# An attention and mixture-of-experts layer: each head's scores in a row group of 32 partitions, the first batch projected straight into it, shift rows in half batches

## The reference

```
x: (8, 256, 128)      16 heads of 8, 8 experts, 2 of them per token
Q, K, V = x @ Wq + bq, x @ Wk + bk, x @ Wv + bv        per batch, 16 heads
attn = softmax(Q K^T / sqrt(8))                        per head, 256 x 256
x = layernorm(x + (attn V) @ Wo + bo)
shared = (silu(x @ sw1) * (x @ sw3)) @ sw2             width 256
gates = the two largest of sigmoid(x @ router_w.T) + bias, normalised
routed = sum over e of gates[e] * gelu(x @ ew1[e]) @ ew2[e]   8 experts, width 128
out = layernorm(x + shared + routed)
```

## Time and profile before

| | |
|---|---|
| median of three runs | 265.02 us (263.12 to 265.13) |
| profiled execution, its span | 261.9 us |
| between its span and the median | 3.1 us |
| PE, PEld busy | 225.9, 158.7 us |
| DVE, ACT, POOL busy | 186.1, 152.3, 119.1 us |
| chain that ended last | PE 59%, DMA 13%, DVE 11%, POOL 6% |

### The profile page before, as it was taken

One profiled execution on the slowest core, in us unless ns is written; L12 is line 12 of the kernel. 1 busy time (PEld: TensorE's weight loads), 2 busy tenths in 40 slices (PEclk: granted clock), 3 DMA queues, 4 the chain that ended last, 5 costly groups with the idle time before them and its releaser, 6 DMA issues.

```text
span 261.9 us, 4502 instructions
## 1 busy us (share of the span) xinstructions
PE 225.9 (86%) x1546; PEld 158.7 (61%) x1546; DVE 186.1 (71%) x370; ACT 152.3 (58%) x292; POOL 119.1 (45%) x186
## 2 busy tenths in 40 slices
PE   1766984999999999994999999997999899999850
PEld 1434854667677677772676766655767576767520
DVE  8953893777969879794269762348567796976953
ACT  1440722576666667663356678866696468665620
POOL 8677381000100007130448988435319977273511
PEclk9995885899999999999589999999979999999995
DMA  7277864405528082476000000069980495792111
GB/s 191 53 92 91 86 69 98 40 11 86 45 53 77 23 85 30 78 53 228 3 0 5 3 5 5 4 108 140 226 143 28 94 147 84 129 161 74 40 40 40
DMA packets 16198, 19.43 MB, mean 74 GB/s; under 512 B 1280, under 2 KB 11712, under 8 KB 16032
## 3 DMA queue, kind: packets, MB, share of 16 engines
q1 hardware_dynamic: 15744, 18.49, 43.4%
q0 software_dynamic: 144, 0.39, 1.0%
q10 hardware_dynamic: 288, 0.27, 0.6%
HBM read 11.22 MB, written 1.11 MB: 47 GB/s over the span
## 4 chain that ended last, share of the span: by engine, by line
PE 59%; DMA 13%; DVE 11%; POOL 6%; issue 5%; ACT 3%; SPq 1%; POOLq 0%; DVEq 0%; ACTq 0%
PE ring L818 17%; PE pv_bank L832 14%; PE max_bank L804 12%; DMA kstack<-gate_scratch 6%; DMA qstack<-top_rows 4%; POOL qstack L522 3%; DVE kstack L629 3%; DVE probs_mem L737 2%; DMA kstack<-qk_parts 2%; ACT qstack L556 1%; PE misc_bank L871 1%; PE misc_bank L882 1%; PE max_bank L788 1%; PE max_bank L789 1%; PE max_bank L790 1%
## 5 line engine op out<-in xcount | busy, mean ns | idle before, releaser
L669 DVE TENSOR_REDUCE top<-max_bank 128x2 f32<-128x512 f32 x128 | 84.0, 684 | 32.9 <-PE max_bank L804 31.7
L569 ACT ACTIVATE probs_mem<-ring 128x512 f32<-128x512 f32 x128 | 73.9, 597 | 43.6 <-PE ring L818 42.4
L818 PE MATMUL ring<-qstack,kstack 128*128 128x256 f32 x256 | 62.9, 331 | 7.7 <-DMA qstack<-top_rows 7.7
L818 PEld LDWEIGHTS ring<-qstack,kstack 128*128 128x128 f32 x256 | 40.5, 199 | 35.9 <-ACT probs_mem L569 25.1
L804 PE MATMUL max_bank<-kstack,qstack 128*128 128x256 f32 x256 | 56.5, 312 | 3.6 <-DMA kstack<-qk_parts 3.3
L804 PEld LDWEIGHTS max_bank<-kstack,qstack 128*128 128x128 f32 x256 | 43.0, 209 | 7.7 <-DMA kstack<-qk_parts 4.1
L832 PE MATMUL pv_bank<-probs_mem,v 128*18 128x256 f32 x512 | 41.3, 397 | 0.0
L737 DVE TENSOR_TENSOR probs_mem<-probs_mem,kstack 128x512 f32<-128x512 f32 x32 | 24.8, 798 | 11.9 <-POOL qstack L522 6.2
L556 ACT CAST qstack<-probs_mem 128x512 fp32r<-128x512 f32 x32 | 19.7, 615 | 16.5 <-DVE probs_mem L737 16.2
L522 POOL TENSOR_TENSOR qstack<-probs_mem,qstack 128x512 fp32r<-128x512 f32 x14 | 19.5, 1392 | 16.2 <-ACT qstack L556 16.1
L473 POOL TENSOR_SCALAR rstd<-mv 128x2 f32<-128x2 f32 x8 | 1.8, 226 | 48.7 <-DVE mv L706 48.5
(11 more groups left out here) (146 smaller groups left out, 386.6 us busy)
## 6 DMA issues: line engine op xcount, KB each, us to landing
kstack<-gate_scratch SPq DMA_DIRECT2D x4, 2048.0 KB, 15.5
kstack<-qk_parts SPq DMA_DIRECT2D x24, 64.0 KB
wf<-w_ffn_dram SPq DMA_DIRECT2D x1, 1408.0 KB, 5.8
qstack<-qk_parts SPq DMA_DIRECT2D x9, 128.0 KB
xs<-x_dram SPq DMA_DIRECT2D x4, 256.0 KB, 5.2
out_dram<-xs SPq DMA_DIRECT2D x4, 256.0 KB, 2.3
kstack<-wf_hi SPq DMA_DIRECT2D x12, 64.0 KB
qstack<-wf_hi SPq DMA_DIRECT2D x6, 128.0 KB
```

The source lines that it names most:

```text
L569: nc.scalar.activation(probs[:, k // 2 % 4, c % 2 * 512:(c % 2 + 1) * 512], ring[k % NRING][:, :], ACT.Exp, scale=SCALE).then_inc(probs_ma ...
L669: dve.tensor_reduce(top[:, half, h:h + 3:2], max_bank[n % NMAX][:, :].rearrange("p (h k) -> p h k", h=2), AX.X, ALU.max).then_inc(max_take ...
L818: ins = mm(ring[k % NRING][:, j * S:(j + 1) * S], kstack[:, s, ab, r, kt * P:(kt + 1) * P], qstack[:, s, r, :], start=True, stop=True)
```

## The change

A head now has a row group of 32 partitions: head group c of four lies at partitions 32c to 32c+25 (24 stacked rows and the two of the shift), without rows of zeros. `qstack` and `kstack` hold all 2048 tokens, four heads (one for each row group) in each of four tiles. A step is one tile: each `ring` bank holds one head with both halves of the keys. Scores of head c alternate with maxima of head c+2, one matmul at a time. `times_v` stands once a tick, behind the second head, as one block. LEAD is 4. The shift is made after every two steps, and SyncE writes it by four transfers.

Batch 0 is projected by weights that the host has laid out in stacked order (`w_first`, three copies of each column): the product lies in the rows of the stack already, ScalarE makes its high part and, by a 0/1 column, the part to subtract, and VectorE writes the stack. Tokens come in units: batch 0, batch 1, then three of 512 tokens. Units 1 to 4 are spread by `spread`, 24 transfers a unit, each to 8 partitions. Units 3 and 4 are projected in ticks 1 and 2, and 7 and 8. The feed-forward weights have memory of their own: they are loaded at tick 1 and split in ticks 4 to 11. The gates of the first two groups are loaded at ticks 21 and 30, into `gates_mem`.

```diff
-NAB, NPAIR = 2, 8
+NT = 4
-LEAD = 6
-NSLOT = 4
+LEAD = 4
+GR = 3 * HD
+KROWS = GR + 2
+UNITS = [(0, S), (S, S)] + [(g * GT, GT) for g in range(1, NG)]
+COPIES = (((0, 1), (HD, 0), (2 * HD, 0)), ((0, 0), (HD, 0), (2 * HD, 1)))
...
-        qstack = sb("qstack", [P, NSLOT, NPAIR, S], F32R)
-        kstack = sb("kstack", [P, NSLOT, NAB, NPAIR, S], F32R)
-
+        qstack = sb("qstack", [P, NT, TOK], F32R)
+        kstack = sb("kstack", [P, NT, TOK], F32R)
...
+        for tick, half, kind, u in ((-5, 0, "xT", 0), (-5, 0, "first", 0), (-5, 1, "first", 1), (-5, 1, "xT", 1),
...
+                                    (1, 0, "xT", 3), (1, 1, "k", 3), (2, 0, "q", 3), (2, 1, "v", 3),
+                                    (7, 0, "xT", 4), (7, 1, "k", 4), (8, 0, "q", 4), (8, 1, "v", 4)):
+            jobs[tick, half].append((kind, u))
+        for n in range(2 * NB):
+            jobs[2 * n + 2 - LEAD, 0].insert(0, ("shift", n))
+        for u, tick in ((2, -1), (3, 3), (4, 9)):
+            for n in range(2 * HPS):
+                jobs[tick + n // 2, n % 2].append(("stack", (u, 1 - n // HPS, n % HPS)))
+        for j in range(HPS):
+            jobs[-4, 0].append(("stack", (1, 1, j)))
+            jobs[-4, 1].append(("stack", (1, 0, j)))
+        jobs[1, 1].append(("load w", 0))
...
-            jobs[max(UP0 + 1, EX0 + NE * (g - 1)), 1].append(("load gates", g))
+            jobs[(21, 30, EX0 + NE, EX0 + 2 * NE)[g], 1].append(("load gates", g))
...
+        def spread(eng, u, i, j):
+
+            t0, n = UNITS[u]
+            for r, part in COPIES[i]:
+                wait_parts(eng, u, i, part)
+                eng.dma_start(stacks[i][32 * j + r:32 * j + r + HD, :, t0:t0 + n].bitcast(F32),
+                              parts[(u - 1) % 2][32 * j:32 * j + 32, i, part, 0:n].bitcast(F32)).then_inc(
+                                  stack_loaded[u] if u > 1 or i else q1_loaded, 16)
...
-                if g < 2:
-                    sp.wait_ge(scores_made, 4 * NSTEP)
+                if g == 0:
+                    sp.wait_ge(qk_lo_made, len(staged) - 2)
+                elif g == 1:
+                    for u in range(1, len(UNITS)):
+                        wait_spread(sp, u)
...
+                        t, q = b % 2 * 2, b // 2 * S
+                        for j in range(HPS):
+                            move(qstack[32 * j + GR:32 * j + KROWS, t:t + 2, q:q + S],
+                                 top_rows[4 * j:4 * j + 4, b % 2, :]).then_inc(shift_loaded[b % 2], 16)
...
+                    if kind == "first":
+                        for i in range(2):
+                            dve.wait_ge(first_lo_made, 2 * b + i + 1)
+                            dve.scalar_tensor_tensor(out=stacks[i][:, b, 0:S], in0=first_bank[b][:, i * S:(i + 1) * S],
+                                                     scalar=b1[:, i * NT + b:i * NT + b + 1], in1=first_lo[:, b % 2, i, :],
+                                                     op0=ALU.add, op1=ALU.subtract).then_inc(first_done, 1)
...
+            def scores(i, c, kt):
+
+                (b, t), r = batch_tile(i), slice(32 * c, 32 * c + KROWS)
+                ins = mm(ring[(4 * i + c) % NRING][:, kt * S:(kt + 1) * S], kstack[r, t, b * S + kt * P:b * S + (kt + 1) * P],
+                         qstack[r, t, b * S:(b + 1) * S], start=True, stop=True)
+                if kt == QT - 1:
+                    ins.then_inc(scores_made, 1)
+
+            def maxima(i, c, qt):
+
+                (b, t), j = batch_tile(i), (c + 2) % HPS
+                r = slice(32 * j, 32 * j + GR)
```

More of the change, by code:

```diff
@@ L49, with build_layer @@
 WCOLS = RW + NE
-def build_layer(nc, x, w_attn, b_rows, w_ffn, out):
+def build_layer(nc, x, w_attn, w_first, b_first, b_rows, w_ffn, out):
     ctx = ExitStack()
@@ L388, in load_gates @@
                 sp.dma_start(gates[g % 2], src.to_broadcast([P, NE, GT])).then_inc(gates_loaded[g % 2], 16)
-            for b in range(3):
-                stack(b)
             for tick, half in HALVES:
@@ L409, in _ @@
                         load_gates(b)
-                if half and step(tick) and tick % SPB == 3 and tick // SPB + NSLOT < NB:
-                    stack(tick // SPB + NSLOT)
-                    if tick // SPB + NSLOT == NB - 1:
-                        for b in (NB - 2, NB - 1):
-                            wait_stack(sp, b)
-                        sp.dma_start(wf[:, :], w_ffn[:, 0:RW]).then_inc(wf_loaded, 16)
             sp.wait_ge(out_stored, 16 * NG)
@@ L459, in _ @@
             for tick, half in HALVES:
-                piece = 2 * (tick - SPB * (NSLOT + 1)) + half
+                piece = 2 * (tick - 4) + half
                 if 0 <= piece < PIECES:
@@ L800, in maxima, with wait_for_maxima @@
+            def wait_for_maxima(i, c):
+                (b, t), n = batch_tile(i), 4 * i + c
+                if b == 0 and c == 0:
+                    pe.wait_ge(first_done, 2 * t + 2)
+                if b and t == 0 and c == 0:
+                    wait_spread(pe, unit_of(b))
                 if n >= NMAX:
                     pe.wait_ge(max_taken, n - NMAX + 1)
-                for j in range(2):
-                    ab, r = heads[2 * (c % 2) + j]
-                    ins = mm(max_bank[n % NMAX][:, j * S:(j + 1) * S], qstack[:, s, r, qt * P:(qt + 1) * P],
-                             kstack[:, s, ab, r, :], start=True, stop=True)
@@ L836, in times_v @@
-                if kt == QT - 1:
-                    ins.then_inc(pv_made, 1)
+                pe.wait_ge(probs_made, 4 * (i + 1))
+                for kt in range(QT):
+                    for j in range(HPS):
+                        ins = mm(pv_bank[32 * j:32 * j + 2 * VW, 0:S],
+                                 v[:, (QT * b + kt) * H // 2 + HPS * n + j, k * VW:(k + 2) * VW],
+                                 probs[:, i % 2, j, kt * S:(kt + 1) * S],
+                                 start=(k == 0 and kt == 0), stop=(k == 1 and kt == QT - 1))
@@ L844, in _ @@
                     if step(tick):
-                        scores(tick, c)
+                        wait_for_scores(tick, c)
+                        scores(tick, c, 0)
                     if step(tick + LEAD):
-                        maxima(tick + LEAD, c)
-                    if step(tick - 1) and c % 2 == 0:
-                        times_v(tick - 1, half)
+                        wait_for_maxima(tick + LEAD, c)
+                        maxima(tick + LEAD, c, 0)
+                    if step(tick):
+                        scores(tick, c, 1)
+                    if step(tick + LEAD):
+                        maxima(tick + LEAD, c, 1)
+                    if step(tick - 1) and c == 1:
+                        times_v(tick - 1)
                 for kind, b in jobs[tick, half]:
```

479 lines of the change are left out of this document (220 added, 259 removed), and 3 rows, old and new, of the table jobs.

## The result

The changed kernel takes 296.27 us (median of four runs, 293.7 to 303.95) against 264.65 for the kernel before (263.12 to 265.13). The prediction was 263.0, in a range of 252 to 275. The profiled execution after has a span of 292.0 us at a mean granted clock of 0.77; before it was 261.9 at 0.93.

A forecast was written before the change was run, and what follows sets the result against it. TensorE was taken as the bound through attention, VectorE close behind. Start 15 us earlier, mostly lost to shift waits: attention ends 2.9 earlier, less 1 for stalls; span 261.9 - 2 = 260, plus 3.1 gives 263.0 us, range 252 to 275.

The forecast's parts named there:

- I take 3.7 a tick with maxima (3.5 to 3.9): Attention loop: a tick, four heads' scores plus later maxima, takes 3.7 us with row groups overlapping, 3.9 without.
- an attention ending after 176: End of attention: predicted at 168.6 us; before 162 or after 176 was to show the prediction wrong.
- The forecast's one term for the clock: Attention: TensorE is slow for a while behind a long stall; 1 us taken off the gain for two such stalls.
- jobs 0.3: Within a tick: 0.3 us for TensorE's other jobs, after the P times V block, in a sum of 3.55.
- The start: Before scoring: first stacks at about 10 us, tick 0 at 27.5 instead of 42.5, 15 us earlier.
- The shifts in the queue: SyncE's DMA queue: stack transfers, weights and gates delay shift rows; waits at ticks 4, 8, 14, and 7 us at 24.
- full engines for 5: DMA at tick 1: 1.4 MB of feed-forward weights fill all 16 engines for 5 us, from about 42 to 47.4.
- the trace agrees: DMA: a transfer to 8 partitions uses 8 engines, said to match busy shares of 0.64 and 0.58 with K transfers.
- A: Whole kernel: early start's gain is kept, gates don't hold shift 12, ticks 3.5 to 3.6: 254 us; chance 0.27.
- B: DMA queue: stack transfers to 8 partitions take over 0.8 us and fall behind: 272 us at 0.96; chance 0.23.
- C: TensorE: row groups don't run side by side, 3.9 us a tick, partly hidden in shift waits: 266 us; chance 0.10.

The follow-up runs named there:

- Masked and thin: Changed kernel with Q in two zero-masked copies (58 and 56 rows), Q transfers from GpSimd, late gates, stack transfers spread, weights in four pieces: 263.23 us, ratio 0.998.
- The clean pair: Changed kernel with mended queue and start, spread stack transfers and split weights, with zero-masked Q copies (58 and 56 rows) 263.23 us, without (26 and 24) 281.27 us.
- The run with halves: Changed kernel with scores over 58 rows of one half of the array and maxima over 56 of the other, side by side: 279.8 and 284.2 us.
- with masks: Changed kernel with zero-masked Q copies, late gates and weights, Q stack transfers from GpSimd, tensor_scalar replaced, stack transfers still in bursts: 272.07 us, ratio 1.032.
- the first masked kernel: Changed kernel with Q in two copies, zeros for every second head (58 and 56 rows), gates and weights late: 277.7 us and three of 288.1 to 290.7.
- one group: Changed kernel with maxima of a pair in the same row group as its scores, so nothing runs side by side: 312.88 us, ratio 1.179.
- fillers: Changed kernel with one extra matmul of 128 rows by 256 columns ahead of each second score matmul, four a tick: 363.3 and 384.6 us.

## Why the prediction was wrong

**The step that failed** is "I take 3.7 a tick with maxima (3.5 to 3.9)". It took every TensorE duration from rows at a clock of 1.00 and never asked whether the new form would be granted it. From tick 4 (scores at 51.8, where 53 was predicted) to the last block of P times V at 199.8, 28 ticks took 148.0 us, 5.29 each with their waits; the prediction had 168.6 - 53 = 115.6, so 4.13. That block began 31.2 us late, where I had said that an attention ending after 176 would prove me wrong. The forecast's one term for the clock, 1 us for "a while" behind long stalls, was the wrong mechanism: the clock fell while TensorE was busy.

**The tick was also mis-sized at full clock.** Masked and thin, with the clock at 1.00 from 60 to 160 us, 20 ticks took 145.72 - 64.78 = 80.9 us by the copies of the top rows: 4.05 each, with one wait of 1.0 in them. The changed kernel itself took 8.03 for two ticks (129.26 to 137.29) at a clock of 0.92. Its blocks of P times V (timeline of TensorE, masked and thin):

```profile
119.64 1.06 PE L822 MATMUL pv_bank<-probs_mem,v 128*18 128x256 f32 x16
...
123.91 1.06 PE L822 MATMUL pv_bank<-probs_mem,v 128*18 128x256 f32 x16
...
127.59 1.06 PE L822 MATMUL pv_bank<-probs_mem,v 128*18 128x256 f32 x16
```

4.27 for the tick that has a shift and the router's six matmuls, 3.68 for the next, where I put "jobs 0.3". My own row gave 0.5 a tick for them, and the shift is there twice as often. As an estimate, (4.05 - 3.7) x 28 is 9.8 us; the remaining 21 of the 31 are then the clock and what it sets off. The clean pair bears that out in size: 16 us, and 5 for the masked kernel's later start.

**The start** was right: maxima at 10.05 (about 10), top rows at 21.7 (20.6), four shift pieces issued from 24.0 to 26.6 (22 to 24.6), tick 0 at 28.2 (27.5).

**The shifts in the queue.** The waits were at the places named but smaller: 4.2 us at tick 4, none at tick 8, 1.3 at tick 14, 1.8 at tick 24 behind the gates instead of 7. The run with halves, at a clock of 0.915, shows why: there it was 5.3, 3.6 at tick 8, 5.0 at tick 14 and 5.5 at tick 24. The mechanism was right and slow ticks covered it. Two of its terms were too small: six stack transfers took SyncE 4.31 us to issue, 0.72 each instead of 0.66, and the weights landed 9.4 us behind their issue, 5.8 before, where I had put full engines for 5. And "the trace agrees" was said too firmly: eight engines of sixteen would be a share of 0.50, and the rows have 0.58 and 0.64 in a measure that goes up to 1.14.

**Rivals.** A (gain kept, 254) didn't come; even the thin kernel only reaches 263, since its ticks are no shorter than the 3.95 of before. B (stack transfers fall behind, 272) has the right sign for another reason: with masks, at clocks of 0.91, the bursts are worth 9 us (272.1 to 263.2). C (no overlap, 266) is refuted by the equal starts. None of the three had the clock in it, and the range was too narrow for that.

## What to carry to other kernels

Fewer rows for each matmul aren't free on TensorE: before costing a packed form at the durations of the full one, try the full-size kernel with only its operands sliced to the new rows; that one edit would have shown 367 us here. Zero rows that look like waste can be what holds the clock: with them the thin kernel runs at 0.91, without them at 0.81. And when ticks get slow, waits for transfers vanish from the profile without being mended: they came back, 21.6 us of them, with the clock of the halves.

## What the runs showed of the hardware

- **The granted clock falls under a busy TensorE.** In the kernel before with 26 rows it was 0.50 in every window from 30 to 210 us, with TensorE 100% busy; with 128 rows it is 1.00. The Trainium skill, TensorE: Matmul & The Clock Gate, section on how HAM oscillation bites in real kernels, gives as the rule that there be no idle gaps; by it the kernel before with 26 rows, which has none, would have kept its 264 us. The measurement decides: it took 367. Mean clocks: 0.64 and 0.71 (26 rows, one group), 0.77 (26 and 24, two groups), 0.84 (34), 0.89 (66), 0.915 (58 and 56 in halves), 0.93 (128). I have no rule that gives these, and not the reason why fillers didn't help. Rows aren't all of it either: masked and thin, the clock was 0.50 from 20 to 35 us with TensorE busy for 14.68 of 15, projections among its work, and 1.00 from 60 to 160 with 88.12 of 100 busy.
- **VectorE's tensor_scalar can wait for GpSimd.** In the changed kernel the 4-column addition of L608, on the path of the first projection, took 3.14 us and ended with GpSimd's clearing (4.47 + 3.14 = 7.61, 2.38 + 5.21 = 7.59; timelines of both):

```profile
2.38 5.21 POOL L399 MEMSET kstack<- 128x6144 f32 x1
...
4.47 3.14 DVE L608 TENSOR_SCALAR b<-b,ones_row 128x4 f32<-128x4 f32 x1
```

As a scalar_tensor_tensor (masked and thin) it took 0.16 under the same clearing:

```profile
4.60 0.16 DVE L633 SCALAR_TENSOR_TENSOR b<-ones_row,b 128x4 f32<-128x4 f32 x1
```

The Trainium skill, GPSIMD Engine Reference, Specifications, says that GpSimd shares its SBUF interfaces with VectorE and contends with its 2-port mode and with instructions of two SBUF inputs. The trace agrees in so far as the tensor_scalar was held. The scalar_tensor_tensor has two such inputs and was not held by this clearing, which only writes; no run here shows it beside a GpSimd instruction that reads.

- **The clock's record can't be relied on at first.** The window from 8 to 12 us of the kernel after shows 1.00, while four maxima at 10.05 took 0.80; four at 22.55, also at 1.00, took 0.51. In the first masked kernel it shows 1.00 from 41 to 46 us with durations of half clock (0.58 and 0.41 for scores). Durations have to be looked at beside it, above all ahead of its first change.
